# A fused residual block on one core: table rows of h and its x difference, here and one row below, written from two transposes, with the x step first and ScalarE scaling the lower part

## What is computed

```
x = x + L0(group_norm(x, 32 groups))
    L0: 3x3 convolution in 8 groups of 64 channels, bias, and a transpose of
        (channel of the group, pixel) into (pixel, channel), read again as NCHW
x = x + L1(group_norm(x, 32 groups))
    L1: h      = relu(bn1(conv1x1(x)))                  512 -> 128 channels
        offset = conv3x3(h)                             18 channels: dy, dx of 9 taps
        val    = for each pixel and tap, h sampled at (y + ky + dy, x + kx + dx):
                 v00*(1-fy)*(1-fx) + v01*(1-fy)*fx + v10*fy*(1-fx) + v11*fy*fx
        out    = relu(bn3(conv1x1(bn2(sum over taps of W_tap * val))))   -> 512
```

## Time and profile before

| | us |
|---|---|
| three runs | 2209.67, 2210.93, 2238.08 |
| median | 2210.93 |
| the profiled execution | 2238.84 |
| its span, first to last instruction | 2236.9 |
| VectorE's `coordinates` of image 0 and of image 15 start at | 120.9 and 2105.3 |

### The profile page before, as it was taken

One profiled execution on the slowest core, in us unless ns is written; L12 is line 12 of the kernel. 1 busy time (PEld: TensorE's weight loads), 2 busy tenths in 40 slices (PEclk: granted clock), 3 DMA queues, 4 the chain that ended last, 5 costly groups with the idle time before them and its releaser, 6 DMA issues.

```text
span 2236.9 us, 31922 instructions
## 1 busy us (share of the span) xinstructions
PE 1810.2 (81%) x10144; PEld 995.9 (45%) x10144; DVE 1395.2 (62%) x3450; ACT 966.5 (43%) x1475; POOL 1182.4 (53%) x1160
## 2 busy tenths in 40 slices
PE   5988787897889788788887888789788878887544
PEld 2544443544545454444444444454444445443221
DVE  5537566574757658466674857668476665846554
ACT  6545353353545435354353545345354443522211
POOL 0046555564556546555564555556455554655664
PEclk9989898897989889888897989899798988988877
DMA  5055665575665656666575665657566575565664
GB/s 181 6 188 154 207 201 179 148 235 173 196 204 169 231 151 219 188 193 194 148 238 164 203 197 181 217 162 238 165 203 199 163 232 156 176 203 160 211 198 154
DMA packets 142933, 412.94 MB, mean 185 GB/s; under 512 B 24614, under 2 KB 25126, under 8 KB 142758
## 3 DMA queue, kind: packets, MB, share of 16 engines
q0 software_dynamic: 92160, 302.06, 45.7%
q1 hardware_dynamic: 50598, 108.71, 13.1%
HBM read 339.37 MB, written 71.30 MB: 184 GB/s over the span
## 4 chain that ended last, share of the span: by engine, by line
PE 47%; DVE 15%; another core or an unknown queue 15%; issue 13%; ACT 5%; POOL 2%; DMA 1%; SPq 1%; ACTq 0%; DVEq 0%; POOLq 0%
PE bank L775 14%; PE bank L757 8%; PE bank L789 8%; DVE sb_rows L567 5%; PE bank L843 4%; PE bank L748 4%; DVE sb_val L575 4%; PE bank L764 3%; PE bank L865 3%; PE bank L808 2%; DVE sb_split L608 2%; POOL sb_rows L332 2%; DVE sb_raw L623 1%; ACT sb_split L406 1%
## 5 line engine op out<-in xcount | busy, mean ns | idle before, releaser
L332 POOL DMA_INDIRECT sb_rows<-table,sb_ridx x1152 | 1178.0, 1023 | 1011.7 <-DVE sb_val L575 440.5
L775 PE MATMUL bank<-sb_split,sb_wg 128*128 128x512 f16 x2304 | 602.5, 409 | 29.6 <-ACT sb_conv_sb L378 20.2
L567 DVE SCALAR_TENSOR_TENSOR sb_rows<-sb_rows,sb_frac 128x256 f32<-128x256 f32 x1152 | 488.3, 479 | 73.6 <-DMA sb_rows<-table,sb_ridx 50.5
L575 DVE SCALAR_TENSOR_TENSOR sb_val<-sb_rows,sb_frac 128x128 f32<-128x128 f32 x1152 | 328.6, 347 | 178.5 <-remote 140.3
L789 PE MATMUL bank<-sb_fold_sb,sb_conv_sb 128*64 128x64 f32 x4096 | 307.1, 287 | 124.6 <-issue 120.3
L775 PEld LDWEIGHTS bank<-sb_split,sb_wg 128*128 128x128 f16 x2304 | 231.2, 104 | 366.3 <-issue 152.9
L616 DVE TENSOR_TENSOR sb_xs<-bank,sb_xs 128x512 f32<-128x512 f32 x128 | 88.3, 690 | 477.4 <-remote 324.6
L757 PE MATMUL bank<-sb_valT,sb_wd 128*128 128x512 f32 x576 | 365.7, 719 | 15.7 <-issue 11.3
L360 ACT ACTIVATE sb_valT<-bank 128x512 f32<-128x512 f32 x288 | 171.2, 595 | 407.5 <-remote 249.1
L789 PEld LDWEIGHTS bank<-sb_fold_sb,sb_conv_sb 128*64 128x64 f32 x4096 | 271.0, 206 | 166.9 <-issue 161.1
L378 ACT ACTIVATE sb_conv_sb<-bank,sb_bias 128x512 f32<-128x512 f32 x256 | 173.6, 685 | 387.7 <-PE bank L775 219.2
(11 more groups left out here) (77 smaller groups left out, 1095.3 us busy)
## 6 DMA issues: line engine op xcount, KB each, us to landing
table<-sb_table_sb SPq DMA_DIRECT2D x144, 256.0 KB
sb_xs<-x SPq DMA_DIRECT2D x64, 512.0 KB
out<-sb_res SPq DMA_DIRECT2D x128, 256.0 KB
sb_rows<-table,sb_ridx POOLq DMA_INDIRECT x1152
sb_rows<-w_group SPq DMA_DIRECT2D x8, 288.0 KB, 9.3
sb_wd<-w_def SPq DMA_DIRECT2D x1, 576.0 KB
sb_w<-w_in SPq DMA_DIRECT2D x1, 256.0 KB
sb_w<-w_out SPq DMA_DIRECT2D x1, 256.0 KB
```

Of the source, the lines that this page charges most:

```text
L332: pool.indirect_dma_start(out=rows[:, (c % RING) * PER + i, :], out_offset=None, in_=tables[u % 2], in_offset=bass.IndirectOffsetOnAxis(ap ...
L567: op = nc.vector.scalar_tensor_tensor(r[:, 0:2 * CH], r[:, 2 * CH:4 * CH], frac[:, parity, half * PER + i, k, 0:1], r[:, 0:2 * CH], ALU.mu ...
L575: op = nc.vector.scalar_tensor_tensor(val[:, c % 2, i * CH:(i + 1) * CH], r[:, CH:2 * CH], frac[:, parity, half * PER + i, k, 1:2], r[:, 0 ...
L775: op = nc.tensor.matmul(pair_ps[half][:, :], wg[:, g, k, :], plane(split1[:, g, :], ky + half * HROWS, kx, HROWS), start=k == 0, stop=k == ...
```

## The change

The table row now holds h, its x difference, and the same two values of the row below. `differences` makes only the x difference. `table_tile` transposes two blocks, ScalarE copies 256 columns, and SyncE stores them twice: to the left half of rows m*128 and on, and to the right half of the rows that stand PITCH above. The last PITCH rows' right half is zeroed once at the start.

The interpolation is cut in two. `along_x` takes the x step on both halves (four operations of 128x256) one slot earlier than the chunk's old slot. ScalarE's new `scale_lower`, last in its slot, multiplies the lower result by fy (four activations of 128x128, SBUF to SBUF). `along_y`, in the chunk's old slot, adds (1-fy) times the upper result (four operations of 128x128); 1-fy is the new small table `rest`. The ring has four chunks, and a ring place is found by `ring_of`.

```diff
     HPLANE = PITCH * (HEIGHT + 3)
-    NDX = ROWS + PITCH
     CH = 128
...
     SHIFT = 7
-    RING = 3
+    RING = 4
     TBUFS = 3
...
         norm1 = sb("norm1", [128, PIX], f32)
-        diff = sb("diff", [128, NDX + 2 * ROWS], f32)
+        diff = sb("diff", [128, ROWS], f32)
         h_sb = sb("h_sb", [128, HPLANE], f32)
         h_split = sb("h_split", [128, 2, HPLANE], f16)
-        table_sb = sb("table_sb", [128, TBUFS, ROW], f32)
+        table_sb = sb("table_sb", [128, TBUFS, ROW // 2], f32)
         rows = sb("rows", [128, RING * PER, ROW], f32)
...
         frac = sb("frac", [128, 2, 8, TAPS, 2], f32)
+        rest = sb("rest", [128, 2, 8 * TAPS], f32)
         ridx = sb("ridx", [128, 2, 8, TAPS], i32)
-        dx, dy, dxy = diff[:, 0:NDX], diff[:, NDX:NDX + ROWS], diff[:, NDX + ROWS:NDX + 2 * ROWS]
         offs_sb = w1_norm
...
         pos_done = sem("pos_done")
+        rest_done = sem("rest_done")
         gathered = [[sem(f"gathered{n}_{i}") for i in range(PER)] for n in range(RING)]
-        lerp_y = sem("lerp_y")
+        lerp_x = sem("lerp_x")
+        scaled = sem("scaled")
+        zero_rows = sem("zero_rows")
         val_done = sem("val_done")
...
-        def landed(image, c):
-            return count(16 * CHUNKS // RING, image, 16 * (c // RING + 1))
+        def ring_of(parity, c):
+            return (c + CHUNKS % RING * parity) % RING
+
+        def landed(image, parity, c):
+            first = CHUNKS * parity
+            done = (first + c) // RING + 1
+            return count(16 * CHUNKS // RING, image, 16 * done - 16 * CHUNKS // RING * parity)
...
                 sp.dma_start(raw_wo, w_off).then_inc(wo_in, 16)
+                sp.wait_ge(zeroed, 2)
+                for table in tables:
+                    sp.dma_start(table[ROWS - PITCH:ROWS, 2 * CH:4 * CH], h_sb[0:PITCH, 0:2 * CH])\
+                      .then_inc(zero_rows, 16)
...
                         sp.wait_ge(tile_out, count(TILES, t, m + 1))
-                        sp.dma_start(tables[u % 2][m * 128:(m + 1) * 128, :], table_sb[:, m % TBUFS, :])\
+                        above = max(m * 128 - PITCH, 0)
+                        sp.dma_start(tables[u % 2][m * 128:(m + 1) * 128, 0:2 * CH], table_sb[:, m % TBUFS, :])\
+                          .then_inc(tile_stored[m % TBUFS], 16)
+                        sp.dma_start(tables[u % 2][above:(m + 1) * 128 - PITCH, 2 * CH:4 * CH],
+                                     table_sb[above + PITCH - m * 128:128, m % TBUFS, :])\
                           .then_inc(tile_stored[m % TBUFS], 16)
...
                 for n in range(TBUFS):
-                    pool.wait_ge(tile_stored[n], count(16 * TILES // TBUFS, t, 16 * TILES // TBUFS))
+                    pool.wait_ge(tile_stored[n], count(32 * TILES // TBUFS, t, 32 * TILES // TBUFS))
                 for c in range(CHUNKS):
...
                         pool.indirect_dma_start(
-                            out=rows[:, (c % RING) * PER + i, :], out_offset=None, in_=tables[u % 2],
+                            out=rows[:, ring_of(u % 2, c) * PER + i, :], out_offset=None, in_=tables[u % 2],
                             in_offset=bass.IndirectOffsetOnAxis(
                                 ap=ridx[:, u % 2, half * PER + i, k:k + 1].bitcast(u32), axis=0),
-                        ).then_inc(gathered[c % RING][i], 16)
+                        ).then_inc(gathered[ring_of(u % 2, c)][i], 16)
...
                     act.wait_ge(h_low, count(1, nxt, 0))
-                    act.wait_ge(diff_done, count(3, nxt, 0))
+                    act.wait_ge(diff_done, count(1, nxt, 0))
+                    act.wait_ge(zero_rows, 32)
                     for half in (0, 1):
...
-                    act.wait_ge(tile_stored[m % TBUFS], count(16 * TILES // TBUFS, t, 16 * (m // TBUFS)))
-                    nc.scalar.activation(table_sb[:, m % TBUFS, :], shuf_ps[m % 2][:, :], ACT.Copy).then_inc(tile_out, 1)
+                    act.wait_ge(tile_stored[m % TBUFS], count(32 * TILES // TBUFS, t, 32 * (m // TBUFS)))
+                    nc.scalar.activation(table_sb[:, m % TBUFS, :], shuf_ps[m % 2][:, 0:2 * CH], ACT.Copy).then_inc(tile_out, 1)
+
+                def scale_lower(image, parity, c):
+
+                    half, k = divmod(c, TAPS)
+                    act.wait_ge(lerp_x, count(CHUNKS, image, c + 1))
+                    for i in range(PER):
+                        q = rows[:, ring_of(parity, c) * PER + i, :]
+                        op = nc.scalar.activation(q[:, CH:2 * CH], q[:, 2 * CH:3 * CH], ACT.Copy,
+                                                  scale=frac[:, parity, half * PER + i, k, 0:1])
+                    op.then_inc(scaled, 1)
...
                         tile_to_sbuf(tile_at(s, 3))
+                    image, back, c = chunk_at(s, -1, t, tail, b)
+                    if image is not None:
+                        scale_lower(image, (u - back) % 2, c)
...
-                def interpolate(image, parity, c):
+                def along_x(image, parity, c):
                     half, k = divmod(c, TAPS)
-                    first = (c % RING) * PER
+                    n = ring_of(parity, c)
                     for i in range(PER):
-                        dve.wait_ge(gathered[c % RING][i], landed(image, c))
-                        r = rows[:, first + i, :]
+                        dve.wait_ge(gathered[n][i], landed(image, parity, c))
+                        r = rows[:, n * PER + i, :].rearrange("p (a b) -> p a b", b=2 * CH)
                         op = nc.vector.scalar_tensor_tensor(
-                            r[:, 0:2 * CH], r[:, 2 * CH:4 * CH], frac[:, parity, half * PER + i, k, 0:1],
-                            r[:, 0:2 * CH], ALU.mult, ALU.add)
-                    op.then_inc(lerp_y, 1)
+                            r[:, :, 0:CH], r[:, :, CH:2 * CH], frac[:, parity, half * PER + i, k, 1:2],
+                            r[:, :, 0:CH], ALU.mult, ALU.add)
+                    op.then_inc(lerp_x, 1)
+
+                def along_y(image, parity, c):
+
+                    half, k = divmod(c, TAPS)
+                    dve.wait_ge(scaled, count(CHUNKS, image, c + 1))
                     dve.wait_ge(valT_done, count(CHUNKS, image, c - 1))
-                    dve.wait_ge(lerp_y, count(CHUNKS, image, c + 1))
+                    dve.sem_inc(dve_passed, 1)
                     for i in range(PER):
-                        r = rows[:, first + i, :]
+                        r = rows[:, ring_of(parity, c) * PER + i, :]
+                        n = (half * PER + i) * TAPS + k
                         op = nc.vector.scalar_tensor_tensor(
-                            val[:, c % 2, i * CH:(i + 1) * CH], r[:, CH:2 * CH],
-                            frac[:, parity, half * PER + i, k, 1:2], r[:, 0:CH], ALU.mult, ALU.add)
+                            val[:, c % 2, i * CH:(i + 1) * CH], r[:, 0:CH], rest[:, parity, n:n + 1],
+                            r[:, CH:2 * CH], ALU.mult, ALU.add)
                     op.then_inc(val_done, 1)
...
                     dve.wait_ge(tile_done, count(TILES, nxt, 0))
-                    nc.vector.tensor_tensor(dx, h_sb[:, 1:NDX + 1], h_sb[:, 0:NDX], ALU.subtract)\
-                      .then_inc(diff_done, 1)
-                    nc.vector.tensor_tensor(dy, h_sb[:, PITCH:PITCH + ROWS], h_sb[:, 0:ROWS], ALU.subtract)\
-                      .then_inc(diff_done, 1)
-                    dve.wait_ge(diff_done, count(3, nxt, 1))
-                    nc.vector.tensor_tensor(dxy, dx[:, PITCH:PITCH + ROWS], dx[:, 0:ROWS], ALU.subtract)\
+                    nc.vector.tensor_tensor(diff[:, :], h_sb[:, 1:ROWS + 1], h_sb[:, 0:ROWS], ALU.subtract)\
                       .then_inc(diff_done, 1)
...
                                             posf[:, :], ALU.subtract).then_inc(pos_done, 1)
+                    dve.wait_ge(pos_done, count(1, t, 1))
+                    nc.vector.tensor_scalar(rest[:, u % 2, :],
+                                            frac[:, u % 2, :, :, 0].rearrange("p a b -> p (a b)"), -1.0, 1.0,
+                                            ALU.mult, ALU.add).then_inc(rest_done, 1)
...
                     if image is not None:
-                        interpolate(image, (u - back) % 2, c)
+                        along_y(image, (u - back) % 2, c)
+                    image, back, c = chunk_at(s, -1, t, tail, b)
+                    if image is not None:
+                        along_x(image, (u - back) % 2, c)
...
                         pe.wait_ge(mid_done, count(2 * QUADS, nxt, m + 1) if a2 else count(2 * QUADS, t, 2 * QUADS))
-                        pe.wait_ge(diff_done, count(3, t, 3))
+                        pe.wait_ge(diff_done, count(1, t, 1))
                     else:
...
                     r = slice(m * 128, (m + 1) * 128)
-                    for i, src in enumerate((h_sb[:, r], dx[:, r], dy[:, r], dxy[:, r])):
+                    for i, src in enumerate((h_sb[:, r], diff[:, r])):
```

## The result

The changed kernel took **2406.99 us**, the median of four runs (2397.07 to 2409.76), where the kernel before took 2216.48 in the four runs shown with it (2209.67 to 2238.08): **1.079** of before by the ratio on record, 95% interval 1.0734 to 1.0845; the two medians divided give 1.086. I had forecast 2257 and a range of 2155 to 2320. It is slower as the likeliest sign said, but by 196 us where I had 46, and 87 us above the range. By the ratio, 1.079 x 2211 = 2386, it would be 66 above it.

The account below looks back on a forecast made before the run. VectorE sets the pace in slots 11 to 15, then waits for a slow TensorE, busiest overall at 81%. Terms -30 + 17 + 3 + 56 = +46 us, against the median 2210.93 giving 2257 us, range 2155 to 2320.

Parts of the forecast that it names:

- the likeliest sign: Direction of the whole change: slower, chance 0.44, against 0.36 for the same and 0.20 for faster.
- (a): TensorE's table tiles: 18 fewer transposes an image, -30 us (bounds 0 and -83).
- (c): ScalarE's table copies, 512 to 256 columns: 0.14 us less each, hidden except the last before `offsets_out`, counted in (e).
- (b): VectorE's slot 17: two differences fewer an image, 43 us of work; gain counted as nothing, at most -43 us.
- (d): ScalarE: 1152 added scaling activations, 1.25 us for four, 21 us a step; not the bound by their sum.
- (e): Slots 2 and 3: scaling ahead of `offsets_out` lengthens TensorE's wait by about 1.05 us an image, +17 us (0 to 20).
- (h): Slots 11 to 15: ScalarE's scaling delays VectorE 10 us, about 8 absorbed; +56 us in all (13 to 99).
- (i): Ring of four: gathers wait for `val` of c-4, data needed a slot earlier, lead unchanged; nothing counted.
- (g): End of the last image: two hand-overs and 1.25 us of scaling not hidden, +3 us.
- (j): Table stored in 288 transfers of 128 KB with 1 KB rows; nothing counted, 6 us a step if time doubled.
- The fall of the clock: Rival: TensorE's clock falls while waiting for `shift_product`, 4.5 us more a step, +109 us, 2320 us; chance 0.15.
- The faster rival: Gathers issued without pause slow TensorE; coming singly they free it and halve slot 3's wait: -71, 2140 us; chance 0.20.

Follow-up runs that it names:

- e_order_scalar: Kernel before with VectorE's first step a slot earlier, idle ScalarE activations waiting for it and the second step waiting for them; table and ring unchanged: 1.082 of before.
- e_gate3: Changed kernel, still four ring buffers, but a chunk's gathers held back until the second step of three chunks ahead is done: 1.0389 of before.
- e_pairs_after: Changed kernel, GpSimd waiting before each even chunk until the last gather of the chunk ahead has landed: 0.9822 of before.

## Why the prediction was wrong

**(a), (c), fewer transposes and shorter copies: right.** -30 us forecast, 38 gained by the two alone. (b) was not tried by itself. (d) is right: four scalings take 1.28 us for 1.25.

**(e), the wait of `offsets_out`: not there.** +17 forecast. TensorE's idle time before the offset product's matmuls is 90.8 us in the whole trace where it was 88.7. The profile now puts 90.7 of it down to ScalarE, and only 32.7 before, but its length is the same: the 1.05 us that ScalarE has more ahead of it don't show, and I did not look into why.

**(h), the coupling: the walk right, its cover wrong.** I put each delay where the trace then showed it and took 10 us for the sum before h_out, of which "about 8 fall into VectorE's pause". That step failed. The intervals of chunks 2 to 7 together grew by 10.5 us (38.3 to 48.8), as walked; that of chunk 8, which holds the pause, shrank only by 3.4 (11.7 to 8.3). The pause was no fixed property of the place before h_out. Before, 12 gathers without a pause lay over it, from the first row below to 1137.91, and the last matmuls of TensorE's shuffle came one or two at a time, as in the second:

```profile
1123.04 1.09 POOL L332 DMA_INDIRECT sb_rows<-table,sb_ridx  x1 [1.53 <-DVE sb_val L575]
```

```profile
1136.54 0.22 PE L789 MATMUL bank<-sb_fold_sb,sb_conv_sb 128*64 128x64 f32 x1 [1.26 <-issue]
```

The gathers' times move with `val`: in the changed kernel `val` comes later there, the gathers come by fours with 1.1 to 4.0 us between them, and the shuffle's 32 matmuls there take 2.14 us in one piece. In all chunks 2 to 8 are 7.1 us longer. I had 4.0 as the middle and 7.1 as the upper end, +99 us: the size was at my bound, though that bound stood for another cause, a product held up as long as before, and that the two agree is luck.

**(i), the ring: the term that broke the range.** I had put it at nothing, with the reason that "the lead stays as it was". Gates of three instead of four are worth 1.0778 to 1.0389, so 3.9%, **some 86 us** on 2211. I asked only whether data would come late. It doesn't: in the changed kernel the gathers of chunks 2 to 8 are all issued 22 to 28 us ahead of the step that writes `val`, against 9 to 20 before, which makes up for the x step that is a slot earlier. What I didn't ask is what GpSimd does with the freedom: it issued five chunks' gathers in one series of 20, in front of each chunk 0 and again at chunk 13. The prediction's last sentence names "GpSimd's issue becoming continuous" among the signs of being wrong; it had no price. With (h) at 99, (g) at its 3, (e) at nothing and (a) at -38, the sum without the ring is +64, or 2275 us; measured for gates of three is 1.0389 x 2211 = 2297. With the ring it is 2361 to 2383, beside 2407 measured and 2386 by the ratio. That this comes close proves little: the terms don't add, as e_order_scalar shows (8.2% for parts of 1.5% and 2.7%).

**(j), smaller stores: small.** Queue 1 takes 12.7% of 2406.5 us for 108.23 MB where it took 13.1% of 2236.9: 306 us of the DMA engines for 293, so 0.8 us more a step, where it would have been 6 had the time of the table's transfers doubled. The gathers of 1 KB are not dearer by the byte: 22.3% of 2262.9 us for 151 MB against 45.7% of 2236.9 for 302. The Trainium skill, Perfetto Trace Analysis, section DMA Optimizations, says that DMAs under 2 KB have a significant overhead for each transfer. In this case the table's rows of 1 KB are at most these 13 us dearer in the whole run, and the gathers of 1 KB not at all; here the measurement decides.

**The rivals.** The fall of the clock is real and smaller than I priced it. In the step shown, TensorE waits 4.23 us ahead of `shift_product`, and from there to the end of the product the clock is mostly at the lower level of 1.2 GHz:

```profile
1224.79 1.11 PE L785 MATMUL bank<-sb_eye_sb,sb_val 128*128 128x128 f32 x4 [4.23 <-DVE sb_val L610]
1226.64 1.86 PE L890 MATMUL bank<-sb_gs,sb_w 128*128 128x1 f32 x8 [0.74 <-DVE sb_gs L685]
1228.37 6.64 PE L880 MATMUL bank<-sb_xs,sb_w_norm 128*128 128x512 f32 x8
```

```profile
1223.60:1236.10 12.50, 10.57 (x38) 6.11 (x40) 8.91 (x22) 8.58 (x16) 7.62 (x8) 0.59 0.63 204
```

The granted clock is 0.59 here, and the product has 6.64 us for the 3.68 of the earlier trace rows. Over the run its group (L880) has 147.9 us; the same group was 118.3 before, so 30 us and not 14 x 4.5 = 63. The faster rival asked the right question, whether TensorE's slowness comes from gathers without a pause, and had half of the answer: in the coupled slots the gathers do come singly, chunk by chunk, but the ring of four packs those ahead of chunk 0 and at chunk 13 into series of 20, where I took it that it would spread them.

## What to carry to other kernels

A pause that is to absorb a delay must be traced to its cause first; if that cause hangs on the very events that are delayed, it moves with them and absorbs less. A deeper ring is not free when nobody needs it: ask what its issuer does with the lead, and look for long unbroken series in its timeline; a wait that breaks them may give more than the change under study. Before splitting a chunk's work over two engines, look at what stands ahead of it in the order of the engine that takes its part over: put it ahead of that engine's long work, or leave it on the busier engine.

## What the runs showed of the hardware

While GpSimd issues gathers without a pause (one per 1.25 us), the signal that a group of TensorE's matmuls is done can come late: an eviction waited 13.56 us for matmuls whose records end 20.8 us earlier, and came free 2.7 us after the series ended. The ends of matmuls in these records are modelled, so they don't tell whether the matmuls or their signal were late. Halving the bytes left most of it (1.0596 for 1.0778); a pause of some 3.5 us after at most eight gathers took the loss away (0.9822 for 1.079). That the times at which gathers start cause a large part of the loss is shown by e_gate3 and e_pairs_after, which change only these. It is not shown that the length of a series is what counts: the pause, which waits for a landing, also keeps fewer gathers in flight, and no run separates the two. By which path gathers hold TensorE back, no run here shows. Nor was the pause tried on the kernel before, whose chunks 1 and 14 (13.1 us each) lie under such series too.
